# Four graph layers on one core: an early flag, a unit matrix from VectorE, weight preparation in pieces, two bf16 products replaced by VectorE passes, and a new order of steps

## Time and profile before

| | |
|---|---|
| time, median of 3 (range) | 518.59 us (518.09 to 518.69) |
| profiled execution, its own time | 518.74 us |
| its span, first to last instruction | 516.9 us |
| busy: PE / PEld / DVE / ACT / POOL | 478.7 / 411.4 / 397.7 / 425.1 / 317.7 us |
| instructions: PE / DVE / ACT / POOL | 3964 / 1558 / 1261 / 717 |
| granted TensorE clock, mean | 0.984 |
| share of 16 DMA engines, main queue | 17.4% |

### The profile page before, as it was taken

The page is one execution under the profiler, slowest core; times in us unless marked ns, Lnnn a source line. Parts: engine busy times, 40 slices in busy tenths (PEclk is TensorE's granted clock), DMA queues, the critical chain, the costliest instruction groups (busy, mean ns, idle before and its releaser), DMA issues. The chain is left out here.

```text
span 516.9 us, 14050 instructions
## 1 busy us (share of the span) xinstructions
PE 478.7 (93%) x3964; PEld 411.4 (80%) x3964; DVE 397.7 (77%) x1558; ACT 425.1 (82%) x1261; POOL 317.7 (61%) x717
## 2 busy tenths in 40 slices
PE   3767899999999999999999999999999999999880
PEld 2556788888888898888888888888888888888660
DVE  3486788889888888889888888888987888766540
ACT  2444999989988888999898888898998988898740
POOL 3054456566766766666666676766676676664562
PEclk9988999999999999999999999999999999999996
DMA  6121101122122211222122221122212200000111
GB/s 188 30 83 41 42 13 53 53 63 61 55 63 62 62 44 37 58 63 63 52 64 62 63 58 31 49 63 62 63 52 64 62 23 22 22 22 22 32 32 30
DMA packets 40220, 26.92 MB, mean 52 GB/s; under 512 B 2641, under 2 KB 39889, under 8 KB 40146
## 3 DMA queue, kind: packets, MB, share of 16 engines
q1 hardware_dynamic: 40146, 26.03, 17.4%
HBM read 17.63 MB, written 8.39 MB: 50 GB/s over the span
## 5 line engine op out<-in xcount | busy, mean ns | idle before, releaser
L744 ACT ACTIVATE p<-p,nmax 128x256 f32<-128x256 f32 x256 | 126.6, 498 | 0.4 <-DVE nmax L941 0.4
L1140 POOL TENSOR_SCALAR x<-y,minus_mean,rstd 128x128 f32<-128x128 f32 x256 | 114.7, 458 | 17.7 <-issue 15.9
L1122 POOL TENSOR_TENSOR rstd<-ve,minus_half 128x2 f32<-128x2 f32 x128 | 101.9, 796 | 0.0
L941 DVE CUSTOM_DVE_ANT_0 p<-ps,neg 128x256 f32<-128x256 f32 x256 | 92.7, 419 | 6.6 <-PE ps L520 6.6
L1115 POOL TENSOR_SCALAR ve<-stats 128x2 f32<-128x2 f32 x128 | 24.7, 193 | 110.8 <-DVE stats L854 105.6
L753 ACT COPY p2T<-ps 128x512 f32<-128x512 f32 x128 | 75.0, 595 | 0.0
L531 PE MATMUL ps<-ident,p 128*128 128x128 f32 x512 | 71.7, 273 | 1.5 <-ACT p L744 1.5
L531 PEld LDWEIGHTS ps<-ident,p 128*128 128x128 f32 x512 | 57.4, 141 | 3.2 <-DVE nmax L941 1.4
L977 DVE SCALAR_TENSOR_TENSOR y<-ps,x 128x256 f32<-128x256 f32 x32 | 13.7, 427 | 56.6 <-PE ps L576 56.6
L854 DVE BATCH_NORM_STATS2 stats<-y 128x6 f32<-128x256 f32 x128 | 53.2, 415 | 2.3
L662 ACT COPY xT<-ps 128x256 f32<-128x256 f32 x96 | 36.6, 382 | 17.6 <-PE ps L400 17.1
(11 more groups left out here) (134 smaller groups left out, 1232.3 us busy)
## 6 DMA issues: line engine op xcount, KB each, us to landing
adj_in<-in_adj_dram SPq DMA_DIRECT2D x32, 256.0 KB, 3.0
xT<-in_xT_dram SPq DMA_DIRECT2D x32, 128.0 KB, 2.8
x_in<-in_x_dram SPq DMA_DIRECT2D x32, 128.0 KB, 3.0
x_aside<-x SPq DMA_DIRECT2D x32, 128.0 KB, 2.2
out_dram<-x SPq DMA_DIRECT2D x32, 128.0 KB, 1.8
l_w<-in_l_w_dram SPq DMA_DIRECT2D x1, 257.0 KB
l_w<-in_l_w_dram SPq DMA_DIRECT2D x1, 256.0 KB
first_w<-in_first_w_dram SPq DMA_DIRECT2D x1, 129.0 KB, 2.2
```

Of the source, the lines that this page charges most:

```text
L744: last = nc.scalar.activation(p2(n)[:, k, a, :], p2(n)[:, k, a, :], ACT.Exp, bias=nmax2(n)[:, k, a:a + 1], scale=-1.0, accum_out=sum2(n)[: ...
L941: last = nc.vector.tensor_tensor_reduce(p2(n)[:, k, a, :], bank("sc2", n, a)[:, k * N:(k + 1) * N], neg2(n)[:, k, :], -1.0, HIGHEST, ALU.a ...
L1122: nc.gpsimd.tensor_tensor(rstd[layer](n), ve[layer](n), minus_half[:, :], ALU.pow)\
L1140: last = nc.gpsimd.tensor_scalar(dst[:, k, 0:D], y_t[layer](n)[:, k, :], minus_mean[layer](n)[:, k:k + 1], rstd[layer](n)[:, k:k + 1], ALU ...
```

## The change

It does the following.

- The comparison of the adjacency maxima moves ahead: flag_a (VectorE), flag (a TensorE product with a column of ones that counts the partitions above 1) and flag_b (VectorE) are steps of the order; the reduction over partitions on GpSimd goes.
- VectorE builds a column index (0 to 127), TensorE transposes one row of it by a product, and a comparison of both gives the unit matrix; lift is made from it. GpSimd sets the zeros and makes not_eye from it.
- setup_later becomes prep_a to prep_d and c_prep_a to c_prep_d, steps between those of graph 0 and 1. The single load step becomes ld_adj, ld_xT, ld_x and ld_w.
- z1 loses its mask product. relu1 becomes a copy times 0.2, lk1 (VectorE) takes the maximum of z and that, e1 subtracts the mask, now from SBUF; neg1 is a step of its own. z1's bank is free after lk1.
- wo2 loses the bias products; y2a adds bo on VectorE, y2b does what y2 did.
- The last three graphs' normalisations of layers two and three run on VectorE.
- Rings: adj 5 (3), eq1 7 (8). All places of PLAN are new; from proj0 (10393) to agg3 (17011) it is 6.6 laps.

```diff
+    "tensor": [("proj0", 10393), ("s2_rows", 10993), ("pT0", 11396), ("prep_a", 11440), ("agg0", 11564),
+        ("prep_c", 11810), ("prep_b", 12220), ("prep_d", 12224), ("xT1", 12236), ("tT", 12376), ("z1", 12497),
+        ("pT1", 12980), ("xw1", 13063), ("agg1", 13230), ("xT2", 13660), ("qk2", 13742), ("sc2", 13919),
+        ("pT2b1", 14152), ("pT2b0", 14239), ("v2", 14267), ("pT2a0", 14331), ("pT2a1", 14721), ("rs_rows", 14953),
+        ("agg2", 15004), ("wo2", 15197), ("xT3", 16038), ("flag", 16694), ("hg3", 16776), ("agg3", 17011)],
+    "vector": [("masks", 10540), ("e0", 10971), ("m0", 11156), ("neg1", 11555), ("s0", 11749), ("r0", 11829),
+        ("y0", 11856), ("b0", 11864), ("lk1", 12704), ("e1", 12828), ("r1", 13288), ("h1", 13298), ("y1a", 13409),
+        ("y1b", 13447), ("b1", 13469), ("eq1", 13525), ("flag_a", 13817), ("e2b", 13907), ("e2a", 13950),
+        ("r2", 14860), ("onT2", 14991), ("y2a", 15234), ("y2b", 15563), ("b2", 15610), ("end_norm2", 15934),
+        ("vals3", 16907), ("y3", 17065), ("b3", 17654), ("end_norm3", 18758), ("flag_b", 22639)],
...
-    "z1": [("b", "e1_ready")],
+    "z1": [("b", "leaky_ready")],
-    "wo2": [("b", "y2_ready")],
+    "wo2": [("b", "y2a_ready")],
...
-                pe.matmul(o, ident_bf[:, :], neg1(n).rearrange("p t n -> p (t n)"), start=True, stop=False)
...
-                    last = pe.matmul(o[:, k * D:(k + 1) * D], ones_bf[:, :], bo_parts[:, :],
-                                     start=False, stop=True)
...
-                nc.scalar.activation(relu(n).rearrange("p t n -> p (t n)"), bank("z1", n), ACT.Relu,
-                                     scale=(1.0 - SLOPE) / SLOPE).then_inc(sem("relu_ready"), 1)
+                nc.scalar.activation(relu(n).rearrange("p t n -> p (t n)"), bank("z1", n), ACT.Copy,
+                                     scale=SLOPE).then_inc(sem("relu_ready"), 1)
...
+            def lk1(n):
+                dve.wait_ge(sem("z_ps"), n + 1)
+                dve.wait_ge(sem("relu_ready"), n + 1)
+                o = bank("z1", n).rearrange("p (t n) -> p t n", t=T)
+                nc.vector.scalar_tensor_tensor(out=relu(n), in0=o, scalar=1.0, in1=relu(n), op0=ALU.mult, op1=ALU.max)\
+                    .then_inc(sem("leaky_ready"), 1)
...
-                    last = nc.vector.tensor_tensor_reduce(p1(n)[:, k, :], o[:, k * N:(k + 1) * N], relu(n)[:, k, :],
-                                                          -SLOPE, HIGHEST, ALU.add, ALU.min, nmax1(n)[:, k:k + 1])
+                    last = nc.vector.tensor_tensor_reduce(p1(n)[:, k, :], relu(n)[:, k, :], neg1(n)[:, k, :],
+                                                          -1.0, HIGHEST, ALU.add, ALU.min, nmax1(n)[:, k:k + 1])
...
+            def y2b(n):
+                dve.wait_ge(sem("y2a_ready"), n + 1)
+                nc.vector.scalar_tensor_tensor(out=y_t[2](n), in0=y_t[2](n), scalar=0.0, in1=x2(n)[:, :, 0:D],
+                                               op0=ALU.max, op1=ALU.add).then_inc(sem("y2_ready"), 1)
...
+            def flag_b(n):
+                dve.wait_ge(sem("excess_ps"), 1)
+                nc.vector.tensor_scalar(excess_flag[:, :], bank("flag", n)[0:1, 0:1], 0.5, None, ALU.is_gt)\
+                    .then_inc(sem("flag_ready"), 1)
...
-            pool.wait_ge(sem("excess_ready"), 1)
-            nc.gpsimd.partition_all_reduce(excess_all[:, :], excess_max[:, :], P, bass.bass_isa.ReduceOp.max)\
-                .then_inc(sem("excess_all_ready"), 1)
```

More of the change, by code:

```diff
@@ L26 @@
 PLAN = {
-    "sync": [("load", -56), ("aside", 7895), ("store", 10433)],
[15 rows of a table removed]
+    "sync": [("ld_xT", 9239), ("ld_adj", 9423), ("ld_w", 10290), ("ld_x", 10634), ("aside", 15609), ("store", 19316)],
[6 rows of a table added]
+        ("c_prep_c", 11874), ("c_prep_d", 12192), ("c_xT1", 12336), ("c_tT", 12450), ("relu1", 12588),
[12 rows of a table added]
 }
 RING = {
[1 row of a table removed]
[1 row of a table added]
     "x1": 3, "xT1": 2, "tT": 2, "xw1": 3, "relu": 2, "p1": 2, "p1T": 2, "h": 2, "hexp": 2,
@@ L51 @@
 }
-FIRST_BANK = {"a": 0, "b": 4}
-WEIGHTS_AFTER = 0
+BANKS = {"a": (0, 1, 2, 3), "b": (4, 5, 6, 7)}
+AT_END = 3
+GRAPHS = {
+    **{step: (0, 1) for step in ("ld_w", "prep_a", "prep_b", "prep_c", "prep_d",
+                                 "c_prep_a", "c_prep_b", "c_prep_c", "c_prep_d")},
+    **{step: (-1, 0) for step in ("flag_a", "flag", "flag_b")},
+    **{step: (0, -AT_END) for step in ("norm2", "norm3")},
+    **{step: (-AT_END, 0) for step in ("end_norm2", "end_norm3")},
+}
 PSUM_USES = {
@@ L83, with graphs_of @@
     "agg3": [("b", "y3_ready")],
-}
+    "prep_a": [], "prep_b": [], "prep_c": [], "prep_d": [],
+    "flag": [("b", "flag_ready")],
+}
+def graphs_of(step, graphs):
+    first, end = GRAPHS.get(step, (0, 0))
+    return range(first if first >= 0 else graphs + first, end if end > 0 else graphs + end)
 def program(engine, graphs):
@@ L90, in program @@
             sorted((place + 1000 * n, k, name, n)
-                   for k, (name, place) in enumerate(PLAN[engine]) for n in range(graphs))]
+                   for k, (name, place) in enumerate(PLAN[engine]) for n in graphs_of(name, graphs))]
 def psum_table(graphs):
-    table, rings = {}, {r: [] for r in FIRST_BANK}
+    table, rings = {}, {r: [] for r in BANKS}
     for step, n in program("tensor", graphs):
         for k, (ring, *_) in enumerate(PSUM_USES[step]):
-            uses = rings[ring]
-            table[step, n, k] = (FIRST_BANK[ring] + len(uses) % 4, uses[-4] if len(uses) >= 4 else None)
+            uses, banks = rings[ring], BANKS[ring]
+            table[step, n, k] = (banks[len(uses) % len(banks)],
+                                 uses[-len(banks)] if len(uses) >= len(banks) else None)
             uses.append((step, n, k))
@@ L623, in _ @@
             run("tensor", {
+                "prep_a": prep_a, "prep_b": prep_b, "prep_c": prep_c, "prep_d": prep_d, "flag": flag,
                 "proj0": proj0, "s2_rows": s2_rows, "rs_rows": rs_rows, "pT0": pT0, "agg0": agg0, "xT1": xT1_, "tT": tT_, "xw1": xw1_, "z1": z1, "pT1": pT1,
@@ L806, in setup @@
             def setup():
-                nc.vector.memset(bias_rows[:, :], 0.0)
-                nc.vector.memset(last_row[:, :], 0.0).then_inc(sem("dve_setup"), 1)
-                nc.vector.memset(ax_row[:, :], 0.0)
-                nc.vector.memset(minus_half[:, :], -0.5)
-                nc.vector.memset(ones_bf[:, :], 1.0).then_inc(sem("dve_setup"), 1)
+                for k in range(8):
+                    last = nc.vector.memset(index[:, k:k + 1], float(k))
+                last.then_inc(sem("index_step"), 1)
+                nc.vector.memset(ones_row[:, :], 1.0)
+                for k, size in enumerate((8, 16, 32, 64)):
+                    dve.wait_ge(sem("index_step"), k + 1)
+                    last = nc.vector.tensor_scalar(index[:, size:2 * size], index[:, 0:size], float(size), None, ALU.add)
+                    last.then_inc(sem("index_step"), 1)
+                nc.vector.memset(lift[:, P - 1:P], 0.0)
                 nc.vector.memset(xw0_all[:, :, :, D + 2:D + 3], 1.0)
@@ L957, in onT2, with y2a @@
                     .then_inc(sem("onT_sb"), 1)
-            def y2(n):
+            def y2a(n):
                 dve.wait_ge(sem("wo_ps"), n + 1)
@@ new lines, in end_norm @@
+            def end_norm(layer, n):
+                dve.wait_ge(sem(f"mean{layer}_ready"), n + 1)
+                dve.wait_ge(sem(f"rstd{layer}_ready"), n + 1)
+                dst = (x3, x4)[layer - 2](n)
+                if layer == 2:
+                    free(dve, "x3", n, "y3_ready")
+                    if n >= RING["x3"]:
+                        dve.wait_ge(sem(f"x3_aside{n % RING['x3']}"), 16 * (n // RING["x3"]))
+                if layer == 3 and n >= RING["x4"]:
+                    dve.wait_ge(sem(f"stored{n % RING['x4']}"), 16 * (n // RING["x4"]))
+                if n == B - AT_END:
+                    dve.wait_ge(sem(f"x{layer + 1}_ready"), n)
+                for k in range(T):
+                    last = nc.vector.tensor_scalar(dst[:, k, 0:D], y_t[layer](n)[:, k, :],
+                                                   minus_mean[layer](n)[:, k:k + 1], rstd[layer](n)[:, k:k + 1],
+                                                   ALU.add, ALU.mult)
+                last.then_inc(sem(f"x{layer + 1}_ready"), 1)
@@ L981, in _ @@
             run("vector", {
[L982 to L983 removed]
+                "masks": masks, "neg1": neg1_, "eq1": eq1_, "flag_a": flag_a, "flag_b": flag_b, "e0": e0, "m0": m0, "s0": s0, "r0": r0, "y0": y0,
+                "b0": lambda n: moments(0, n), "lk1": lk1, "e1": e1, "r1": r1, "h1": h1, "y1a": y1a, "y1b": y1b,
                 "b1": lambda n: moments(1, n), "e2a": lambda n: e2(0, n), "e2b": lambda n: e2(1, n), "r2": r2,
[L985 removed]
+                "onT2": onT2, "y2a": y2a, "y2b": y2b, "b2": lambda n: moments(2, n), "vals3": vals3, "y3": y3,
```

(1 more changed line is left out.)

188 lines of the change are left out of this document (94 added, 94 removed), and 25 rows, old and new, of tables (PLAN, RING).

## The result

The changed kernel took 569.23 us (median of 4 runs, 567.98 to 569.83) against 518.64 us for the kernel before on the same chip (4 runs, 518.09 to 518.99): a ratio of 1.097, 95% interval 1.095 to 1.100. I had said slower, and 546 us (508 to 560); the sign was right, the size too small by 23 us. The profiled execution took 569.83 us, its span 568.0.

What follows compares the result with a forecast made beforehand. TensorE bounded the old kernel; its lap of 14.06 plus waits of 1.15, 0.24 and 0.20 gave 15.65. Start 38, 3 x 14.44, 28 x 15.65, tail 25.1 and 1.84 outside the span: 546.4 us, range 508 to 560.

Steps and rivals of the forecast that it cites:

- (1): TensorE between sc2 and agg2: agg2's bank waits for vals3, which VectorE runs behind e2b; 1.15 us per lap.
- (2): TensorE between xT2 and qk2: waits for ScalarE's copy, 0.90 against 0.66 of own work; 0.24 us per lap.
- (3): TensorE between xw1 and z1: ScalarE's unbroken work takes 5.68 against TensorE's 5.48; 0.20 us per lap.
- fourth chain: agg1, GpSimd's normalisation of layer one, then xT2: could add up to 0.35 us per lap; counted as 0.
- TensorE's own lap: TensorE's work per lap without waits: 14.06 us, after removing 0.38 of mask and bias products.
- The forecast of 3.21 from sc2 to agg2: Time from sc2's start to agg2 with vals3 behind e2b's four heads: 3.21 us, against 2.06 of TensorE's own.
- I take none of it: Layer one's reciprocal root on GpSimd: the up to 0.35 us per lap from its long kind was left out.
- The rival with chance 0.09 (lap 16.0, 556.2): GpSimd's layer-one normalisation chain binds too, with the slow root every lap: lap 16.0, 556.2 us, chance 0.09.
- The new forms of e1 and y2b: VectorE instructions with two SBUF inputs, excluding GpSimd's SBUF reads: would make the 1.065 us root more frequent.
- I leave them at 14.44: The first three laps, which have no vals3 yet, were kept at the old lap of 14.44 us each.
- the 1.6 for normalising on VectorE: Tail: last normalisations at some 0.6 instead of 0.9 on VectorE, with GpSimd freed, save about 1.6 us together.
- VectorE's added work: lk1 and y2b add 1.05 us per lap to VectorE, giving 13.7, below TensorE's 14.06: nothing for the lap.

Runs made afterwards that it cites:

- e1_behind_e0: old_order with VectorE's e1 moved from place 4438 to 4453, so that it runs after e0: 496.31 us, ratio 0.957.
- Experiments 3 and 4: Changed kernel with vals3, the adjacency passes or both moved: 545.03, 562.34, 538.91 us; then layer one's root made a multiplication in the first and last: 534.49, 533.92 us.
- old_order: All edits of the changed kernel, with every step of PLAN back at its place in the kernel before: 514.99 us, ratio 0.991.
- short_root_moved: both_moves with GpSimd's reciprocal root of layer one replaced by a multiplication: 533.92 us, ratio 1.029.
- vals_first: Changed kernel with vals3 moved from place 16907 to 16890, ahead of e2b on VectorE: 545.03 us, ratio 1.048.
- both_moves: Changed kernel with eq1 at 13891, masks at 10895 and flag_a behind them, and vals3 at 16897, all ahead of e2b: 538.91 us, ratio 1.038.
- short_root: vals_first with GpSimd's reciprocal root of layer one replaced by a multiplication: 534.49 us, ratio 1.030.

## Why the prediction missed

Of the 23.4 us, 21.7 are in the laps, 1.4 in the tail, 0.3 before the first sc2. What TensorE stands in a lap can be read off as the distance of two starts, less the same distance in e1_behind_e0, where it never stands:

```
place                         predicted   measured
sc2 to agg2 (1)                 1.15        1.17
xT2 to qk2 (2)                  0.24        0.28
before z1 (3), 0.09; behind it   0.20        0.21
agg0 to xT2 (fourth chain)      0           0.39
agg3, qk2's halves              0           0.18
sum                             1.59        2.23
```

With 14.04 the right column makes 16.27, for a lap of 16.24 to 16.26. Of the 1.17 in its first row only 0.95 is the wait for vals3, for with vals3 early sc2 to agg2 still takes 2.20. The other 0.22 stands behind rs_rows (0.35 to the next start, where 0.22 is usual) and behind s2_rows (0.31): I had put that stretch at 2.06.

**What held.** TensorE's own lap (14.06; e1_behind_e0 has 14.04) and the distances behind stalls (1) to (3), each to 0.04, though the wait for vals3 itself was put 0.2 too large. The forecast of 3.21 from sc2 to agg2 was 3.15. lk1 took 0.69 (taken: 0.65). First sc2 38.33 (38; kernels with almost the same start scatter by 3.5 us, so that a hit to 0.3 is partly luck), exp0(0) at 9.05 (9.7), and the flag ends 0.1 after the last normalisation. VectorE as a whole is not the bound at 83%.

**The step that failed: "I take none of it".** The root of layer one took 1.07 in the shown lap, not 0.71, and xT2 waits for it; the chain has nothing to spare. That is 0.39 x 28 = 10.9 us. I held against it that it needs the slow kind every lap, as if kinds were drawn by chance, because I read the earlier trace rows as "mostly takes 0.711, at times 1.065". But a periodic schedule puts the same neighbours together each lap, and it did so before, too. A lap has four roots, one for each layer, and in the kernel before 23 of the 101 took over 1.0 us, 14.1 to 14.75 apart: always layer one's, which stood beside the passes over the adjacency (VectorE, then GpSimd with another layer's root for comparison):

```profile
254.72 0.42 DVE L849 TENSOR_SCALAR eq<-adj_in 128x512 f32<-128x512 int32 x1
255.39 0.42 DVE L840 TENSOR_SCALAR neg<-adj_in 128x512 bf16<-128x512 int32 x1
```

```profile
254.78 1.06 POOL L1122 TENSOR_TENSOR rstd<-ve,minus_half 128x2 f32<-128x2 f32 x1
261.52 0.72 POOL L1122 TENSOR_TENSOR rstd<-ve,minus_half 128x2 f32<-128x2 f32 x1
```

So the slow root was there in every lap of the steady state. What the new order took away is the slack behind it: before, layer one's normalisation ended at 256.9 and xT2 started at 257.66. Experiments 3 and 4 show both that the chain binds and that these passes stretch it; old_order, where two of them stand beside the root, has it at 0.92. The rival with chance 0.09 (lap 16.0, 556.2) was the nearest to what happened.

The new forms of e1 and y2b, which I suspected, did not make the slow kind more frequent: between 100 and 460 it is 22 of 88 roots in the new order with the old code, which has neither, and 22 of 89 in the changed kernel. The Trainium skill ("SBUF — State Buffer", "Who interferes with whom") would have led further than I took it. I used its sentence on two SBUF inputs; it also names `tensor_scalar` in its 2-port modes as holding the pair, and `tensor_reduce` as never contending on this chip. The rows agree: L892, L879 and L885 go over 512 columns in 0.42, where TENSOR_REDUCE needs 0.67, and GpSimd is stretched beside the former (ve 0.29, root 1.07, and x 1.41, this one beside y2b too) and not beside the latter (0.19 and 0.23).

**"I leave them at 14.44"**, for the first three laps, also failed: they took 16.39, 15.14 and 15.15. vals3 is absent from them, but (2), (3), the fourth chain and the small gaps are not (14.04 + 1.06 = 15.1). The first has a wait of its own: xw1's bank waits for e2a until 42.52. Together 3.4 us. The small gaps, 0.18 x 28 = 5.0 us, come one by one at 0.07 and 0.11; the trace names no releaser, and their cause stays open. The remaining 2.4 of the 21.7 are the 0.07 by which the first three rows of the table were short, and a few long laps (16.6, 16.7 and 16.8). The same reading accounts for the 1.0 of short_root_moved: 0.28 before qk2, 0.23 before and in xw1, 0.20 before and behind z1, 0.22 between sc2 and agg2, 0.18 in the small gaps (1.11 together, less 0.07 by which agg0, agg1 and hg3 are shorter).

The tail was 1.4 longer, and there the mis-sized term is the 1.6 for normalising on VectorE. From the last sc2 to the end of the last normalisation it took 22.98 (541.51 to 564.49), against 23.15 before: 0.2 gained. old_order has the same edits without the new order's waits on vals3 and the root, and needs 23.4, so those waits don't explain it; why the shorter passes gained so little stays open. What follows the last normalisation took 3.5 (taken: 3.6).

**VectorE's added work**, lk1 and y2b, was put at nothing for the lap because VectorE as a whole stays below TensorE. That held in the new order, where they meet idle time. In the old one it fails: old_order's VectorE is idle for 9% of the time, and e0 is 0.8 late in its place all the same. The warning that stood beside it ("hardly any slack for waits that its order imposes") was the better half of that sentence. The edit that makes e0 late there is lk1: without it the lap is 14.26.

## What to carry to other kernels

Price an order by each hand-over's due time on the engine that waits, the ring of PSUM banks included, before any instruction is priced: one step placed 17 thousandths of a lap too late cost 28 us here, and another, 15 thousandths too early, 19. In a periodic schedule an instruction that is "sometimes" slow is worth splitting by its place in the lap before anything else: here a minimum, median and maximum over all four roots hid that one of them was slow every time. Then it must be priced with its neighbours in the new order, for it meets the same ones each lap. After any edit that lengthens one engine's queue, look for the first result behind it that frees a bank, and move that forward; here this turned 515 us into 496.

## What the hardware showed that I had not expected

The stretching goes both ways, and reaches into passes that were never slow before. GpSimd's normalising passes (duration min/median/max in ns, between 100 and 460) in the new order with the old code, and in the changed kernel:

```profile
L1142 POOL TENSOR_SCALAR x<-y,minus_mean,rstd x172: 440/453/501, 108.5 to 458.2; 128x128 f32<-128x128 f32 x172
```

```profile
L1214 POOL TENSOR_SCALAR x<-y,minus_mean,rstd x176: 445/458/1011, 102.7 to 456.0; 128x128 f32<-128x128 f32 x176
```

The slow ones are 19 of the 176 (18 of them at about 0.7 us), and all stand beside m0 (L914), which reads two SBUF tiles and which both kernels have. So no new instruction is needed for it, only a new meeting: in the new order with the old code four passes ran from 296.59 to 298.36 and m0 began at 298.95. In the changed kernel (GpSimd, then m0's second half, which took 0.60 for its usual 0.42):

```profile
317.49 2.04 POOL L1214 TENSOR_SCALAR x<-y,minus_mean,rstd 128x128 f32<-128x128 f32 x4 [0.17 <-issue]
```

```profile
319.21 0.60 DVE L914 CUSTOM_DVE_ANT_0 p<-p,neg 128x256 f32<-128x256 f32 x1
```

So too e1's first head (L949, both inputs in SBUF) took 0.57 in old_order while GpSimd normalised, its second 0.41.

At the start the granted clock differs between kernels that are almost the same: 0.65 over 27 to 41 us in vals_first and 0.66 in short_root_moved, 0.99 in both_moves and 1.00 in short_root, with a first sc2 at 40.1, 40.1, 36.7 and 36.5. That is a scatter of 3.5 us, larger than some of the effects looked for, so laps were compared and not total times. The tails differ in the same way: 28.4 in the three kernels whose clock fell to 0.84 and 0.50 there, 26.5 in the changed kernel.
